# Products that nobody reads on TensorE, ahead of and in the waits of the first group of a fused cross-attention, recurrence and FFN kernel

## The reference

```python
x = x + xattn(layernorm(x), ctx)     # 8 heads of 64; ctx has 257 rows of 192 channels for each batch
x = x + attn(layernorm(x))           # state = (1 - w) * state + k v^T, read by r, 4 heads of 64
x = x + ffn(layernorm(x))            # low rank: 256 -> 64 -> 1024 gelu -> 64 -> 256
```

## Time and profile before

| | us |
|---|---|
| median of 3 runs (lowest, highest) | 1005.36 (1003.62, 1005.92) |
| the profiled execution's own time | 1006.33 |
| its span, first to last instruction | 1004.5 |
| PE busy in it | 965.0 |
| DVE, ACT, POOL busy in it | 614.3, 583.1, 373.0 |

### The profile page before, as it was taken

How to read it: one execution, slowest core, us unless ns; L and a number is a source line. 1 busy time by engine, 2 the same in 40 slices (tenths; PEclk the granted TensorE clock), 3 DMA queues, 4 the chain that set the end, 5 groups by cost and what they waited for, 6 DMA issues and landing times.

```text
span 1004.5 us, 23095 instructions
## 1 busy us (share of the span) xinstructions
PE 965.0 (96%) x8840; PEld 812.0 (81%) x8840; DVE 614.3 (61%) x1285; ACT 583.1 (58%) x1439; POOL 373.0 (37%) x484
## 2 busy tenths in 40 slices
PE   4889999999999999999999999999999999998987
PEld 3667888888888888888888888888888888887875
DVE  3665758475575837557583755758375575837352
ACT  3555646566574656657465665746566574655331
POOL 1332525244352524435252443525244352524130
PEclk9899999999999999999999999999999999999999
DMA  8314231321322132232213213221321322122000
GB/s 292 97 48 125 59 114 47 97 77 58 107 73 91 47 96 78 58 107 76 86 49 97 77 58 107 69 91 51 96 78 59 106 75 76 49 86 58 12 1 22
DMA packets 58011, 79.00 MB, mean 79 GB/s; under 512 B 10288, under 2 KB 39856, under 8 KB 57904
## 3 DMA queue, kind: packets, MB, share of 16 engines
q1 hardware_dynamic: 56192, 76.38, 24.8%
q10 hardware_dynamic: 1712, 1.16, 0.4%
HBM read 73.05 MB, written 4.46 MB: 77 GB/s over the span
## 4 chain that ended last, share of the span: by engine, by line
PE 80%; DVE 8%; ACT 5%; issue 4%; POOL 2%; DMA 0%; DVEq 0%; POOLq 0%
PE gb L353 15%; PE scores L412 8%; PE acc L443 7%; PE gb L476 6%; PE scores L416 6%; PE acc L439 6%; PE ptp L426 6%; PE gb L537 5%; PE acc L444 5%; PE gb L586 3%; DVE xn L801 3%; PE gb L576 3%; PE gb L385 2%; ACT probs L651 2%; DVE probs L814 2%
## 5 line engine op out<-in xcount | busy, mean ns | idle before, releaser
L1040 POOL TENSOR_TENSOR t_l<-raw_t,t_h 128x516 fp32r<-128x516 f32 x128 | 167.3, 1307 | 206.9 <-PE scores L416 170.9
L651 ACT ACTIVATE probs<-scores,small 128x257 f32<-128x257 f32 x256 | 119.4, 472 | 149.8 <-DVE small L807 149.6
L807 DVE TENSOR_REDUCE small<-scores 128x2 f32<-128x514 f32 x128 | 88.3, 690 | 117.8 <-PE scores L416 117.3
L1049 POOL TENSOR_TENSOR ptm<-probs,head 128x32 f32<-128x32 f32 x128 | 35.2, 275 | 277.3 <-DVE probs L814 277.3
L814 DVE TENSOR_TENSOR probs<-probs,small 128x514 f32<-128x514 f32 x128 | 101.7, 794 | 4.4
L426 PE MATMUL ptp<-ident,probs 128*128 128x128 f32 x512 | 79.9, 279 | 13.3 <-DVE probs L814 11.9
L443 PE MATMUL acc<-pt,raw_n 128*128 128x256 f32 x256 | 89.6, 432 | 0.0
L412 PE MATMUL scores<-t_h,qk_h 128*128 128x258 f32 x256 | 84.1, 328 | 2.2 <-DVE qk_l L861 2.2
L662 ACT ACTIVATE pt<-ptp 128x512 f32<-128x512 f32 x128 | 77.3, 604 | 13.7 <-PE ptp L426 11.8
L439 PE MATMUL acc<-pt,raw_n 128*64 128x128 f32 x1024 | 83.2, 283 | 0.4 <-ACT pt L662 0.4
L1113 POOL TENSOR_TENSOR rstd<-ve,half 128x2 f32<-128x2 f32 x48 | 33.4, 696 | 124.4 <-ACT t_h L658 71.6
(11 more groups left out here) (168 smaller groups left out, 2758.2 us busy)
## 6 DMA issues: line engine op xcount, KB each, us to landing
raw_t<-in_ctx_t SPq DMA_DIRECT2D x128, 258.0 KB, 3.0
raw_n<-in_ctx_n SPq DMA_DIRECT2D x128, 192.0 KB, 2.4
xb<-in_x SPq DMA_DIRECT2D x16, 256.0 KB, 4.3
vsp<-tail_values SPq DMA_DIRECT2D x256, 2.0 KB
out<-ob SPq DMA_DIRECT2D x16, 256.0 KB, 2.8
xin<-in_x SPq DMA_DIRECT2D x15, 256.0 KB, 2.9
khat<-in_wq ACTq DMA_DIRECT2D x1, 512.0 KB, 4.5
wv<-in_wv SPq DMA_DIRECT2D x1, 512.0 KB, 6.4
```

Source lines behind the costliest of these rows:

```text
L651: go(probs[n % 2][:, r, 0:L], scores[:, r, 0:L], ACT.Exp, bias=nmax[:, r:r + 1], accum_out=rsum[:, r:r + 1]).then_inc(s["exp_ready"], 1)
L807: v_.tensor_reduce(nmax[:], scores[:, :, 0:L], AX.X, ALU.max, negate=True)\
L1040: p_.tensor_tensor(t_l[m % 2][:], raw_t[m % RING][:], t_h[m % 2][:].bitcast(F32), ALU.subtract)\
```

## The change

WARM = 22 products go to the very start of PE's stream, ahead of its wait for the identity, as soon as DVE has set a tile to 1.0; FIRST_SCORES = 10 products go behind `score(0)`; and BUSY gets four entries for group 0: 5 behind XT, 3 behind Qa1, 7 behind Qb, 6 behind WZ. `stay_busy` loses its wait, writes to `ptp` and not to `scores`, and takes both operands from `ones`, which is the tile `psp` under another name. The fills of the "behind" part can now be followed by products as well.

```diff
+WARM, FIRST_SCORES = 22, 10
+BUSY = {("XT", 0): 5, ("Qa1", 0): 3, ("Qb", 0): 7, ("WZ", 0): 6,
+        ("Y2", OLD): 4, ("XT2", NEXT): 5, ("H2", OLD): 2, ("Y3", OLD): 1, ("O2", NEXT): 3, ("Y2", NEXT): 9,
...
+        ones = psp[:].rearrange("p b s -> p (b s)")
...
             def stay_busy(count):
-                pe.wait_ge(s["exp_ready"], 2 * B)
                 for k in range(count):
-                    mm(scores[:, 0, 0:256], ident[:], v1[:, 0:256], start=True, stop=True)
+                    mm(ptp[:, 0], ones[:, 0:P], ones, start=True, stop=True)
+
+            pe.wait_ge(s["ones_ready"], 1)
+            stay_busy(WARM)
             pe.wait_ge(id_in, 16)
...
                         score(n + 1)
+                    if n + 1 == 0:
+                        stay_busy(FIRST_SCORES)
...
                     for name, g in behind:
                         steps[name](g)
+                        if (name, g) in BUSY:
+                            stay_busy(BUSY[name, g])
...
+            v_.memset(ones, 1.0).then_inc(s["ones_ready"], 1)
             v_.memset(half[:], -0.5).then_inc(s["half_ready"], 1)
```

More of the change, by code:

```diff
@@ L54 @@
 BEGINNING = {1: ["XT"], 2: ["q0", "q2", "q1", "q3"], 3: ["Qa0"], 5: ["Qa1"], 6: ["Qb"]}
-BUSY = {("Y2", OLD): 4, ("XT2", NEXT): 5, ("H2", OLD): 2, ("Y3", OLD): 1, ("O2", NEXT): 3, ("Y2", NEXT): 9,
+WARM, FIRST_SCORES = 22, 10
+BUSY = {("XT", 0): 5, ("Qa1", 0): 3, ("Qb", 0): 7, ("WZ", 0): 6,
+        ("Y2", OLD): 4, ("XT2", NEXT): 5, ("H2", OLD): 2, ("Y3", OLD): 1, ("O2", NEXT): 3, ("Y2", NEXT): 9,
         ("XT3", NEXT): 1, ("Pf", NEXT): 1, ("H2", NEXT): 3, ("Qf", NEXT): 1}
@@ L238, in build @@
         bank_drained = [sem(f"bank_drained{i}") for i in range(BANKS)]
-        names = ("half_ready zeros_ready small_ready scores_ready nmax_ready exp_ready probs_ready pt_ready ptev_ready "
+        names = ("half_ready ones_ready zeros_ready small_ready scores_ready nmax_ready exp_ready probs_ready pt_ready ptev_ready "
                  "acc_ready pc_ready ptm_ready var0_ready var1_ready var2_ready rstd0_ready rstd1_ready rstd2_ready xn0_ready xn1_ready xn2_ready high_act_ready high_pool_ready low_ready qk_h_ready xb_ready ob_ready "
```

## The result

| | before | after |
|---|---|---|
| median of 16 runs (lowest, highest), us | 1005.53 (1003.62, 1007.32) | 1008.68 (1005.77, 1010.5) |
| ratio after / before, 95% interval | | 1.0024 [1.0014, 1.0034] |
| profiled execution: own time, span | 1006.33, 1004.5 | 1009.01, 1006.6 |
| PE busy in it | 965.0 | 982.9 |

What follows compares the result with a forecast made beforehand. PE, busy 96% of the span, was taken to bound the kernel. A 1.6 us loss at the start less 0.7 at WZ gave +0.9: 1007.2 on the profiled execution, 1006.2 on the median, range 1003.0 to 1008.8.

Steps and rivals of the forecast that it cites:

- the likeliest case: Whole kernel: clock rises 3.8 to 6.5 us after PE's start, sum +0.9 us, median 1006.2, read as same; chance 0.49.
- rival (A): Starting products: the clock rises later and the change is slower, 1007.8 on the median, deciding from +2.0; chance 0.27.
- (A)'s sign: Start of PE's stream: the 22 products ending beyond 13.8 would show the later clock rise.
- What a product costs: Each dummy product: two records, 0.427 us at the full clock and 0.85 at the lower level.
- Rival (B): Start: a product is short or the 22 are over by 8.3, so -5.4 us, about 1000; chance 0.06.
- The end of the 22: Start: the 22 products run from 1.15 to 12.89, so XT starts 4.4 us late.
- The q's: Group -1: 24 q's at the full clock take 2.82 us, the clock giving back 2.27 us.
- turn_probs(0) and turn_probs(1): First group: they start at 31.11 and 35.84, 3.03 and 1.61 us late, released at turn_probs(0) by PE's own products.
- The excess of the fills: Behind Qb and score(0): the 7 products cost 0.68 us beyond their cover, the 10 cost 1.22.
- WZ: Behind WZ: six products start turn_probs(5) 0.46 us late, but the clock stays up, giving 0.7 us earlier.
- At no cost: The dropped wait, the bank ptp, the memset on DVE and the new operands cost nothing.
- The last groups: Last groups: the new operands of their 30 products change no duration.

Runs made afterwards that it cites:

- the late fills: The changed kernel plus 4 products behind XT2 and 4 behind H0 of the last group but one; 1008.93 us, ratio 1.003 against the kernel before.
- the cut and the two late fills: Changed kernel with 10 products at the start, fills cut to their waits, 4 more products behind both XT2 and H0 of the last group but one; 1000.99 us, ratio 0.9957.

## Why the prediction was right, and what it mis-sized

Slower by 0.9 us was forecast (1006.2, range 1003.0 to 1008.8); the median came out at 1008.68, at the upper end, and the ratio says 0.24% slower where the likeliest case was a slowdown of 0.09% that reads as no change. None of the cases happened as it was written. The slowdown has the size at which rival (A) decides (a sum of +2.0), but its place holds only a part of it: the time until the rise was 6.0 us, inside the 3.8 to 6.5 that I had given to the forecast itself, and XT started at 13.58, short of the 13.8 that was to be (A)'s sign. The rest are small sums of the same sign and what happens late in the kernel, which I hadn't priced. Step by step:

- **What a product costs**: right. 0.427 us at the full clock, 0.85 at the lower one, two records each; 22 more cost 9.5 us in time by the medians. Rival (B) is out. An estimate from the low-clock gap that the Trainium skill gives (TensorE: Matmul & The Clock Gate, Back-to-back issue gap) has the 22 products last at most 4.7 us. They took 12.39, so that gap, counted once for a product, doesn't hold for these float32 products.
- **The end of the 22**: 12.89 forecast, 13.58 measured. The rise was mis-sized: 12.39 - 22 x 0.427 = 3.0 us of surplus, which is half of a cold time of 6.0 us, where I took 4.7 and gave 3.8 to 7.2 as ends. That is 0.65 of the 0.69.
- **The q's**: forecast 2.82, measured 3.15, since the first record of a group takes 0.30 to the next one and the hand-over to Qa 0.21. Such starts of a group (0.1 to 0.2 us each) are missing in my sum at score(0) and at the 10 products too: 26.52 to 28.07 is 1.55 where I had 1.31, and the 10 take 4.42, not 4.27.
- **turn_probs(0) and turn_probs(1)**: 31.11 and 35.84 forecast, 32.49 and 37.17 measured. The lateness against before is 2.9 us, not 1.6: about 0.5 of the 1.3 by the clock's rise as it reached the q's, the rest by the group starts. That turn_probs(0) would be released by PE's own products was right: no bracket at 32.49.
- **The excess of the fills**: right in kind. Cutting Qb's, score(0)'s and XT's by 2, 4 and 2 products brought batch 1 forward by 1.93 us (29.38 to 27.45); 0.68 + 1.22 were forecast. That the sums agree so well is in part luck: 1.51 of it came behind batch 0, at score(0)'s products, and XT started 0.31 later in the profile with the cut fills (8.79 against 8.48).
- **WZ**: 0.7 forecast, 0.68 measured (2.94 late at batch 1, 2.26 at batch 7). The 0.46 by which six products outlast the wait came too: with four products 1.14 are won there (from 4.05 to 5.19 ahead of before).
- **At no cost**: right, ratio 1.0001.
- **The last groups**: taken as the same in both. They aren't from run to run. In the profile the fall at 914.8 raises the lateness from 2.46 at batch 120 to 3.77 at batch 127, by 1.3 us; then the kernel before pays for its own fall at 978, and 2.1 us are left in the span. In the timed runs the 16 of the changed kernel split by their mean granted clock: six at 1.000 take 1005.77 to 1006.82, ten at 0.998 or 0.997 take 1008.53 to 1010.5. The fall at 914.8 explains 1.3 of the more than 2 us between the two parts; the rest is not shown. The 73 runs of the kernel before taken beside the experiments split too: 29 at 0.993 have a median of 1005.05, 31 at 0.992 one of 1006.77 (the other 13 stand at 0.990 and 0.995). The forecast of 1006.2 is about what the changed kernel takes when no fall comes late; the median lies in the other part. That this agrees is luck in part: the 1006.2 is summed on a profile of before that has the fall at 978 in it, and the start lost 2.3 us by batch 7 where 0.9 was forecast.

What stays open: whether the late falls come more often in the changed kernel than before. The mean clock counts all cold stretches together, so the runs don't say in how many executions of the kernel before one came at batch 123, and taking that fall away left the time where it was. Open too is the drift of up to 1 us between batch 7 and batch 120.

## What to carry to other kernels

Dummy products that raise the clock have to be over when the first real operand is there: count them from the price of a product at both levels, and take the latest rise seen. Here 10 at the start and fills no larger than the waits they stand in turned +0.24% into -0.37%. Look at the bracket on the first real instruction behind them: as long as it still waits for its operand the products are free, and where the bracket is gone, each further one is carried to the end in full. A PE busy share that rises with the time is a warning, not a result.

## What the runs showed of the hardware that I had not expected

- The rise of the clock from the first product on varies from profile to profile of the same stream. Counted as twice the surplus of the starting products over 0.427 us each, it took 6.0 us in the changed kernel, 4.0 with the 22 alone, 3.8 with 44, 6.5 with the late fills, and from 3.2 to 6.3 in the six kernels with 10 (3.2 with 10 alone, 4.3, 4.5, 4.7, 5.4, and 6.3 with the cut and the two late fills). With 6.3 the 10 just last until xn is there: XT starts at 8.60, and the bracket at it is gone.
- A wait of 1.5 to 2 us can be enough for a fall, and the same wait in another execution passes without one: the 1.93 us behind WZ brought the clock down in the profile of before and not in that of the 22 alone; the 1.87 us at batch 123 did it after and not before.
- PE can be busy without a pause and its clock still fall: at 64 records of 64x32 it fell in six of twelve profiles of the same step, in five of them within 1 us behind the records, in one among them. With two 128x256 products put in it stayed up in the profile, which one profile can't show to be their doing.
